# Weight splitting of w1 and w2 moved to GpSimd, bulk weight loads to the SyncE queue, and the gate multiplies to VectorE

## What is computed

```python
xn = _layernorm(x)
q, k, v = xn @ Wq * dk**-0.5, xn @ Wk, xn @ Wv          # 4 heads, dk 256, dv 512
gk = log_sigmoid(xn @ Wgk1 @ Wgk2 + bgk2) / 16
#   scan over tokens, per head:  S = S * exp(g_t)[:, None] + k_t v_t^T ;  o_t = q_t @ S
o = o * rsqrt(mean(o*o) + eps) * g_norm_weight * silu(xn @ Wg)
x = x + o @ Wo + (relu(xn @ w1 + b1) @ w2 + b2)         # w1 [1024, 4096], w2 [4096, 1024]
```

## Time and profile before

| | us |
|---|---|
| median of the 2 runs shown (5228.5 and 5773.11) | 5500.8 |
| the profiled execution | 5223.09 |
| its span on the slowest core (core 7) | 5221.5 |
| its shortest core (core 5) | 5187.5 |
| PE busy | 3454.7 |
| DVE busy | 1322.4 |
| ACT busy | 788.9 |
| POOL busy | 481.2 |

### The profile page before, as it was taken

How to read it: one execution, slowest core, us unless ns; L and a number is a source line. 1 busy time by engine, 2 the same in 40 slices (tenths; PEclk the granted TensorE clock), 3 DMA queues, 4 the chain that set the end, 5 groups by cost and what they waited for, 6 DMA issues and landing times.

```text
span 5221.5 us, 51725 instructions; the slowest of 8 cores (5187.5 to 5221.5 us)
## 1 busy us (share of the span) xinstructions
PE 3454.7 (66%) x17640; PEld 1990.2 (38%) x17640; DVE 1322.4 (25%) x1944; ACT 788.9 (15%) x2034; POOL 481.2 (9%) x1014
## 2 busy tenths in 40 slices
PE   1000565775996666775997766765997756765997
PEld 0000434543442434543443435544443435544443
DVE  3333122122222122122222122122222122122222
ACT  4333111111000211011000211011000211011000
POOL 2222100000000000000000000000000000000000
PEclk7555787887998777887998777887999777887999
DMA  6999511110323110110323110210323111200222
GB/s 181 249 268 281 182 33 33 65 44 28 106 94 113 53 33 33 65 34 31 109 93 113 54 36 33 65 33 33 102 96 116 47 40 37 65 21 33 81 96 78
DMA packets 176739, 431.37 MB, mean 83 GB/s; under 512 B 22737, under 2 KB 55633, under 8 KB 176482
## 3 DMA queue, kind: packets, MB, share of 16 engines
q0 software_dynamic: 67584, 234.92, 13.9%
q1 hardware_dynamic: 72034, 159.57, 10.5%
q10 hardware_dynamic: 36864, 33.57, 2.5%
HBM read 352.48 MB, written 75.50 MB: 82 GB/s over the span
## 4 chain that ended last, share of the span: by engine, by line
PE 63%; DMA 12%; DVE 11%; issue 6%; ACT 5%; POOL 2%; ACTq 0%; DVEq 0%; SPq 0%; POOLq 0%
PE pb L899 13%; PE pb L549 6%; PE pb L940 5%; PE pb L946 4%; PE pb L943 4%; DVE k_sils L719 4%; PE pb L807 3%; PE pb L792 3%; PE pb L840 3%; DMA h_v<-w_l 3%; PE pb L654 2%; PE pb L844 2%; PE pb L847 2%; PE pb L657 2%; PE pb L660 2%
## 5 line engine op out<-in xcount | busy, mean ns | idle before, releaser
L549 PE MATMUL pb<-t_xnfh,w_wqh 128*128 128x512 bf16 x256 | 98.1, 383 | 494.1 <-DMA w_wql<-wq_lo 494.1
L940 PE MATMUL pb<-w_wgh,f_h1h 128*128 128x512 bf16 x1024 | 387.6, 379 | 52.3 <-DVE k_gg L908 37.9
L899 PE MATMUL pb<-t_xnfh,w_wvh 128*128 128x512 bf16 x1024 | 388.0, 379 | 29.4 <-DVE t_attn L963 29.4
L899 PE MATMUL pb<-t_xnfh,w_wvl 128*128 128x512 bf16 x1024 | 388.1, 379 | 0.0
L899 PE MATMUL pb<-t_xnfl,w_wvh 128*128 128x512 bf16 x1024 | 388.0, 379 | 0.0
L946 PE MATMUL pb<-w_wgh,f_h1l 128*128 128x512 bf16 x1024 | 387.9, 379 | 0.0
L943 PE MATMUL pb<-w_wgl,f_h1h 128*128 128x512 bf16 x1024 | 387.8, 379 | 0.0
L807 PE MATMUL pb<-h_v,k_khtm 128*128 128x256 f32 x512 | 171.8, 467 | 236.3 <-ACT k_khtm L764 164.5
L787 PE MATMUL pb<-h_v,k_p 128*128 128x256 f32 x256 | 115.8, 599 | 309.3 <-ACT k_otm L696 205.2
L654 PE MATMUL pb<-w_wvh,t_xnfh 128*128 128x256 bf16 x1024 | 287.2, 281 | 28.7 <-ACT h_spf L585 28.7
L963 DVE SCALAR_TENSOR_TENSOR t_attn<-pb,t_attn 128x512 f32<-128x512 f32 x224 | 146.9, 687 | 587.4 <-PE pb L946 575.0
(11 more groups left out here) (151 smaller groups left out, 5393.0 us busy)
## 6 DMA issues: line engine op xcount, KB each, us to landing
w_wvh<-w_hi POOLq DMA_DIRECT2D x64, 512.0 KB, 3.6
w_wvl<-w_lo POOLq DMA_DIRECT2D x64, 512.0 KB, 3.6
w_wgh<-w_hi POOLq DMA_DIRECT2D x64, 512.0 KB, 3.6
w_wgl<-w_lo POOLq DMA_DIRECT2D x64, 512.0 KB, 3.6
t_x<-x SPq DMA_DIRECT2D x32, 512.0 KB, 4.5
h_v<-w_l SPq DMA_DIRECT2D x64, 256.0 KB, 13.3
h_g<-w_l SPq DMA_DIRECT2D x64, 256.0 KB, 13.2
w_wvh<-wv_hi POOLq DMA_DIRECT2D x32, 512.0 KB, 3.6
```

Source lines behind the costliest of these rows:

```text
L549: last = t.matmul(pb[bk][:, 0:PW], wgt[:, k * 128:(k + 1) * 128], mov[k][:, sl], start=first, stop=(k == 7 and wgt is wl))
L899: last = t.matmul(pb[bank][:, 0:tile_tok], w_ap, mov[k][:, 0:tile_tok], start=first, stop=(k == 7 and lo_pass))
L940: last = t.matmul(pb[bk][:, 0:512], hh, wgh_cs[jpi][:, wsl], start=(slot == 0), stop=False)
```

## The change

The first 128 split jobs stay as they are. The 128 jobs of w1 and w2 are done by GpSimd alone: it issues the load into the same landing tiles, copies to the high part, subtracts to the low part, and issues both stores; the parts are staged in the four slots of `h1h` and `h1l`. The loads of `load_vg` and `load_w12` are issued by SyncE. The multiplies of `emit_gates` are done by VectorE.

```diff
@@ in emit_split, for each job
+            if mn in ("w1", "w2"):
+                sw = i % 4
+                hcol = h1h[:, sw * 512:(sw + 1) * 512]
+                lcol = h1l[:, sw * 512:(sw + 1) * 512]
+                hkey = f"h1h_{sw}"; lkey = f"h1_{sw}"
+                OP("gpsimd", lambda g, srcp=srcp, lb=lb: g.dma_start(
+                   out=lb, in_=srcp),
+                   writes=[lbk], dma=True, stream=f"spl12_{i % n_land}")
+                OP("gpsimd", lambda g, lb=lb, hcol=hcol: g.tensor_copy(
+                   out=hcol, in_=lb),
+                   reads=[lbk], writes=[hkey])
+                OP("gpsimd", lambda g, lb=lb, hcol=hcol, lcol=lcol:
+                   g.tensor_tensor(out=lcol, in0=lb, in1=hcol,
+                   op=ALU.subtract),
+                   reads=[lbk, hkey], writes=[lkey])
+                OP("gpsimd", lambda g, hip=hip, hcol=hcol: g.dma_start(
+                   out=hip, in_=hcol),
+                   reads=[hkey], writes=hwr, dma=True, stream=f"s12h{sw}")
+                OP("gpsimd", lambda g, lop=lop, lcol=lcol: g.dma_start(
+                   out=lop, in_=lcol),
+                   reads=[lkey], writes=lwr, dma=True, stream=f"s12l{sw}")
+                continue
@@ in load_vg (and in the same way for both loads of load_w12)
-        OP("gpsimd", lambda g, s=s: g.dma_start(out=bh[half][:], in_=hi[s]),
+        OP("sync", lambda ss, s=s: ss.dma_start(out=bh[half][:], in_=hi[s]),
...
-        OP("gpsimd", lambda g, s=s: g.dma_start(out=bl[half][:], in_=lo[s]),
+        OP("sync", lambda ss, s=s: ss.dma_start(out=bl[half][:], in_=lo[s]),
@@ in emit_gates (and in the same way for kt)
-                    OP("gpsimd", lambda g, c2=c2, jt=jt, x=x: g.tensor_tensor(
+                    OP("vector", lambda v, c2=c2, jt=jt, x=x: v.tensor_tensor(
                        out=qt[x][:, c2 * C:(c2 + 1) * C],
```

More of the change, by code:

```diff
@@ L345, in emit_split @@
             sslot = i % 12
+            hwr = [f"scr_{mn}_h{sslot}"]
+            lwr = [f"scr_{mn}_l{sslot}"]
+            if mn in ("w1", "w2"):
[20 more added lines that the diff above has]
+                continue
             hcol = hi_all[sslot // 4][:, (sslot % 4) * 512:(sslot % 4) * 512 + 512]
@@ L348, in emit_split @@
             hkey = f"splh{sslot}"; lkey = f"spll{sslot}"
-            lastp = (i == len(split_jobs) - 1)
             OP("sync", lambda s, srcp=srcp, lb=lb: s.dma_start(out=lb, in_=srcp),
@@ L360, in emit_split @@
                reads=[lbk, hkey] + srd, writes=[lkey])
-            hwr = [f"scr_{mn}_h{sslot}"]
-            lwr = [f"scr_{mn}_l{sslot}"]
             OP("scalar", lambda sc, hip=hip, hcol=hcol: sc.dma_start(
@@ L407, in load_w12 @@
         b = jp % 2
-        OP("gpsimd", lambda g, jp=jp, b=b: g.dma_start(out=bh[b][:], in_=hi[jp]),
+        OP("sync", lambda ss, jp=jp, b=b: ss.dma_start(out=bh[b][:], in_=hi[jp]),
            reads=SCRK(mat), writes=[f"{key}hcs{b}"], dma=True, stream=f"{strm}{b}")
-        OP("gpsimd", lambda g, jp=jp, b=b: g.dma_start(out=bl[b][:], in_=lo[jp]),
+        OP("sync", lambda ss, jp=jp, b=b: ss.dma_start(out=bl[b][:], in_=lo[jp]),
            reads=SCRK(mat), writes=[f"{key}lcs{b}"], dma=True, stream=f"{strm}{b}")
```

## The result

The changed kernel is slower: the ratio of its time to the time before is 1.0856, with a 95% interval of 1.0804 to 1.0907 (5,639.8 to 5,700.3 us against 5,203.5 to 5,230.0 us). I read core 2 of the changed kernel, 5,633.0 us at a granted clock of 0.816, and set it against core 2 of the kernel before, 5,201.0 us at 0.831. The difference is +432 us.

What follows compares the result with a forecast made beforehand. The prediction took the split stage to be bound by DMA, with TensorE waiting 494.1 us for the first q weights. From 5223.1 us, + 651 - 168 + 28 gave 5734, stated as 5735 us; range 5540 to 6050.

Steps and rivals of the forecast that it cites:

- Start of the stage: GpSimd in the split: it reaches job 128, the first of w1 and w2, at about 312 us.
- part 1: First 128 split jobs: unchanged, and the first q loads go out at 314.5 us instead of 553.8.
- Price of a job: Jobs 128 to 255 on GpSimd: nothing overlaps, 7.37 us each, 943 us for 128; bounds 6.3 and 11.1 us.
- The allowance of 15 us for collisions: Split on GpSimd: 15 us added because SyncE's loads of q, k, v, g and wo collide with a few jobs.
- Who waits: VectorE's v and g evacuations in tile 0 wait for GpSimd's reads of the landing tiles; everything behind shifts +651 us.
- the mark: VectorE evacuation of block 1 of the second half in tile 0: at 1275 us instead of 624.
- Gates: Gate multiplies on VectorE, no longer behind GpSimd's loads: 10.5 us a head gained, -168 us over 16; bounds 0 and -230.
- x: Tile ends: the residual's x load stands behind load_vg on SyncE, 9.5 us in each of three tiles, +28 us.
- The landing tiles hold nothing: Rival: tile 0 starts at 315 and the split hides behind its heads; 5100 us, 3 in 100.
- GpSimd is quicker: Rival on the w1 and w2 jobs: 6.3 us a job, 138 us less, 5596 us; 25 in 100.
- slower: Rival: GpSimd's loads wait behind its own stores, 9.4 us a job, 5996 us; 20 in 100.
- The gates give nothing back: Rival: the multiplies stand ahead of the mask on VectorE and wait for ScalarE; 5903 us, 7 in 100.

Runs made afterwards that it cites:

- e5_xland: Changed kernel, but the w1 and w2 jobs land in the four halves of the two x buffers instead of the v and g tiles; ratio to before 0.9711.
- e6_prefetch: Changed kernel with its landing tiles kept, each w1 or w2 job's load issued three jobs ahead; ratio to before 1.0046.
- e2_gates: Kernel before with only the gate multiplies moved to VectorE, loads staying on GpSimd; ratio to before 0.9678.
- e10_both: Kernel before with gate multiplies on VectorE and v, g, w1, w2 loads on SyncE, split as before; ratio to before 0.9718.
- e9_nocomp: As e7_xland_pre, without GpSimd's copy and subtraction in the w1 and w2 jobs, zeros stored instead; 4,813 us.
- e7_xland_pre: Changed kernel with w1 and w2 jobs landing in the x buffers and their loads issued three jobs ahead; 4,839.6 and 4,844.2 us.

## Why the prediction was right

**Reading.** The first line of the prediction reads the DMA slices as 9 to 11 tenths in the first five of forty; they are 6, 9, 9, 9 and 5. No term hangs on it.

**Start of the stage.** Predicted 312 on the profiled core; on core 2 the first job starts at 293.4, where the last store of wo ended at 302.4 before. Nine microseconds were gained; the likely reason, not tried by itself, is that no load of w1 follows close behind job 127 any more. I had called part 1 unchanged.

**Price of a job.** Predicted 7.37, measured 6.96. Term by term: the three issues 0.55 + 0.56 + 0.54 = 1.65 (1.62 predicted); the wait for the load 3.30 (3.3); the subtraction 1.147 (1.25); the copy 0.609 (0.9); waits on its own results, what is left, 0.25 (0.3). The copy is the term that was mis-sized: I took the middle of 0.515 and 1.25 us, and it lies near the lower row, the memset of the same size. The allowance of 15 us for collisions was not needed on top. The stage ended at 1,184 instead of 1,270.

The load's wait was the term with the widest bounds, 2.6 to 6.7 us, and it decided the size of the loss. It fell on the value that was reasoned from two rows, a landing without traffic and this engine's own stores ahead of it. That the mean fits to the second digit is luck: single waits run from 2.5 to 7.4 us, the first ten, beside the loads of q to wo, have a mean of 4.9, and no run takes the stores away alone. The estimate of 2.6 us from the Trainium skill, DMA: Bandwidth & Descriptors, section Anatomy of one DMA — SWDGE (gpsimd) path, was 0.7 us below it; the page's rule has nothing for stores queued just ahead.

**Who waits.** Predicted a VectorE wait of over 800 us at the evacuations of v and g, with TensorE standing too; measured 801.9 and 822.6. e5_xland shows that it is the landing tiles that make it: with other tiles and the same job price it is gone. How long it is, the job's price decides: 406.1 us in e6_prefetch. Predicted +651 at the mark, measured +583.3. On core 2 my terms would have given 659; of the 76 us between, 9 are the start, 128 x 0.41 = 52 the job and 15 the allowance.

**Gates.** Predicted 10.5 us a head. Chunk 0 of a head in the changed kernel, VectorE and then TensorE (tile 0, head 0):

```profile
1200.66 0.41 DVE L624 TENSOR_TENSOR_SCAN k_at<-c_ones,h_spf 128x128 f32<-128x128 f32 x1
...
1203.34 0.28 DVE L800 TENSOR_TENSOR k_p<-pb,c_triu 128x128 f32<-128x128 f32 x1
```

```profile
1203.98 1.10 PE L808 MATMUL pb<-h_v,k_p 128*128 128x256 f32 x4 [3.50 <-DVE k_p L800]
1204.92 1.89 PE L813 MATMUL pb<-st_S,k_qt 128*128 128x256 f32 x8
1206.64 1.03 PE L828 MATMUL pb<-h_v,k_khtm 128*128 128x256 f32 x4
```

The khtm product stands right behind the output matmuls, as I had it; before, it came 10.35 us after them. It takes 1.03 us where it took 2.04. The mask is 2.0 us later than with two scans alone, as worked out. From the scan to the scores of chunk 1 it is 10.3 us; in the head of the earlier trace rows it was 20.6, so 10.2 us are gained where I had 8.7. In chunk 1 the way from scores to output went from 4.85 to 3.92 us, the 0.9 of the prediction. By the marks, less than that comes out at the end: the twelve heads of tiles 1 to 3 went from 2,391.2 to 2,262.1 us, 10.8 a head, and on core 2 all sixteen gave back 50.3 + 120.1 = 170 us; predicted 10.5 and 168.

**x.** Predicted 9.5 us a tile, 28 us; measured 17.6 us in the three feed-forward blocks (1,160.0 against 1,142.4), 5.9 a tile, and 6.1 between e2_gates and e10_both. The mechanism is there, and its size was set 10 us too high. The residual adds at the end of tile 0 in the timeline of VectorE in the changed kernel are

```profile
2185.15 1.23 DVE L1005 TENSOR_TENSOR t_attn<-t_attn,t_x 128x1024 f32<-128x1024 f32 x1 [7.07 <-DMA t_x<-x]
...
2190.89 1.23 DVE L1005 TENSOR_TENSOR t_attn<-t_attn,t_x 128x1024 f32<-128x1024 f32 x1 [3.11 <-DMA t_x<-x]
```

Block 0 waits 7.07 us for x where it waited for none, block 1 some 2 us less than the 5.07 of before, so the two together lose some 5 us where I had counted the whole way of one x load. It goes on to the next tile: ScalarE's wait for x there is 165.3 us in all against 146.8 before, 6.2 us a tile.

**Sum.** Predicted 651 - 168 + 28 = +511, a ratio of 5735 / 5223 = 1.098. Measured +583 - 151 = +432 on core 2, a ratio of 1.0856. Of the 79 us between, 68 lie in the first term (the job's price and its start) and 11 in the others: on core 2 the heads give 170, x and the end take 19, and 170 - 19 = 151. So the terms hold one by one, and none hides another's error: the copy, the allowance and x were each set too high.

On core 2, tile 1 to the end takes 3,423.0 us in the changed kernel and 3,407.3 in e10_both, with the same code. In the means over cores 0 to 3 the difference is 4.2 us (3,412.9 and 3,408.7), less than the cores of one execution differ, so nothing is left here to explain.

**The rivals.** "The landing tiles hold nothing" was a matter of fact and false, as e5_xland shows by making it true. I had priced it at 5,100 us with a wait of 256 us for the split in front of the feed-forward block; the wait was 207.7 us and the time 5,050. "GpSimd is quicker" by 6.3 us a job and "slower" by 9.4 lie on both sides of the 6.96. "The gates give nothing back" falls with e2_gates.

## What to carry to other kernels

Work moved off a DMA-bound stage onto an engine that issues its own load, waits for it, computes and stores has the full landing in every step: 6.96 us against 3.69 with three loads ahead. Before moving such work behind other work, follow the buffers that it borrows to the next writer, since landing elsewhere, at the same job price, took away all of the 608 us that this move cost (e5_xland); three loads ahead in the same tiles took away 423 of them (e6_prefetch). And a queue in which short compute stands behind loads that wait for one another costs its consumers the loads; moving either one cures it, and the loads then push back whatever stands behind them on the new queue.

## What the runs showed of the hardware

VectorE instructions that take both inputs from SBUF take longer while GpSimd computes from SBUF: 293 to 526 ns for a 128x128 multiply, 418 to 645 ns for a scan, 752 to 927 ns for a three-input product of 128x512 (means over 310 to 560 us of e9_nocomp and of e7_xland_pre). Those with an input in PSUM do not change (copy 425 ns, state update 748 and 747 ns). GpSimd's DMA issues alone, at 4.82 us a job, do nothing of the kind (e9_nocomp). In 8 of the 22 qt multiplies beside the split of e7_xland_pre a subtraction of GpSimd was under way when the multiply started, and each of these ends 0.145 to 0.148 us after that subtraction, however long it still ran. The Trainium skill, SBUF — State Buffer, section Who interferes with whom, says that an instruction of VectorE with two SBUF inputs contends with one of GpSimd that reads SBUF, and calls the port pair that the two engines share "an exclusive lock". The trace agrees with both, by the multiplies that end with the subtraction, and gives the price here as 21 us over the four heads of tile 0 (722.7 against 701.8 us).

A copy with conversion from fp32 to bf16 on GpSimd takes 0.609 us for 128x512, about half of a two-input subtraction of that size (1.147 us).
